# Making the normalised rows on GpSimd instead of VectorE in a two-layer gated cross-attention block

## The reference

```python
x = x + tanh(g_xattn[0]) * _L0_xattn_ref(_layernorm(x), ctx_512, ctx_512, Wc, bc)     # 16 heads of 16, then Wc
x = x + tanh(g_ffn[0])   * _L0_ffn_ref(_layernorm(x), w_gate, w_up, w_down)           # silu*up, 2:4 sparsified, down
x = x + tanh(g_xattn[1]) * _L1_xattn_ref(_layernorm(x), ctx_512, ctx_512)             # 32 heads of 8
x = x + tanh(g_ffn[1])   * _L1_ffn_ref(_layernorm(x), gate_w, gate_b, w1, w2, w3, sw1, sw2, sw3)  # 8 experts, top 2
```

## Time and profile before

| | |
|---|---|
| median of 3 runs | 654.88 us (650.46 to 657.46) |
| profiled execution | 653.18 us, its span 651.4 us |
| granted TensorE clock, mean | 0.982 of full speed |
| busy: TensorE, VectorE, ScalarE, GpSimd | 582.7, 471.9, 436.8, 238.8 us |
| instructions | 10817 |

### The profile page before, as it was taken

How to read it: one execution, slowest core, us unless ns; L and a number is a source line. 1 busy time by engine, 2 the same in 40 slices (tenths; PEclk the granted TensorE clock), 3 DMA queues, 4 the chain that set the end, 5 groups by cost and what they waited for, 6 DMA issues and landing times.

```text
span 651.4 us, 10817 instructions
## 1 busy us (share of the span) xinstructions
PE 582.7 (89%) x3552; PEld 450.7 (69%) x3552; DVE 471.9 (72%) x1152; ACT 436.8 (67%) x812; POOL 238.8 (37%) x498
## 2 busy tenths in 40 slices
PE   0654788999999999999999999999999999999886
PEld 0332576777878777777878787777778786767675
DVE  4361878686969788796969697887969696966444
ACT  3251655677786877677777868776777778678952
POOL 5340444261534334251515343351515152341120
PEclk9975999899999999999999999999999999999999
DMA  8752007000000000000000000000000000000000
GB/s 258 217 183 75 4 17 109 18 9 18 14 21 10 22 15 18 10 18 17 17 19 15 20 9 22 14 15 12 18 9 11 8 11 10 12 7 2 10 8 17
DMA packets 24694, 21.44 MB, mean 33 GB/s; under 512 B 9872, under 2 KB 23680, under 8 KB 23744
## 3 DMA queue, kind: packets, MB, share of 16 engines
q1 hardware_dynamic: 21984, 13.04, 7.8%
q0 software_dynamic: 1888, 4.87, 2.5%
q10 hardware_dynamic: 768, 2.85, 1.5%
HBM read 12.61 MB, written 5.24 MB: 27 GB/s over the span
## 4 chain that ended last, share of the span: by engine, by line
PE 66%; ACT 13%; POOL 7%; DVE 6%; issue 5%; DMA 2%; SPq 1%; DVEq 0%; POOLq 0%; ACTq 0%
PE bank L742 12%; PE bank L750 12%; PE bank L745 12%; PE bank L789 8%; PE bank L832 7%; PE bank L744 5%; PE bank L821 4%; ACT L658 3%; POOL rt L547 3%; ACT L696 2%; ACT pt L658 2%; PE bank L818 2%; PE bank L819 2%; DMA k0a<-down_hi 2%; PE bank L911 1%
## 5 line engine op out<-in xcount | busy, mean ns | idle before, releaser
L658 ACT ACTIVATE pt<-bank 128x512 f32<-128x512 f32 x192 | 109.4, 603 | 10.1 <-PE bank L821 5.5
L1092 DVE TENSOR_REDUCE mx<-bank 128x4 f32<-128x512 f32 x128 | 86.1, 684 | 8.3 <-PE bank L789 7.4
L707 ACT ACTIVATE ht_hi<-bank 128x512 fp32r<-128x512 f32 (+1 forms) x96 | 50.4, 543 | 61.4 <-PE bank L750 60.8
L742 PE MATMUL bank<-w_r,at_hi 128*128 128x352 f32 x256 | 88.4, 346 | 3.4 <-DVE work L1200 0.9
L456 POOL TENSOR_SCALAR a_ve<-a_mv 128x1 f32<-128x1 f32 x32 | 9.1, 284 | 214.2 <-DVE a_mv L1062 213.3
L745 PE MATMUL bank<-w_r,at_lo 128*128 128x352 f32 x256 | 82.2, 323 | 0.0
L1137 DVE SCALAR_TENSOR_TENSOR work<-bank,cw,work 128x176 f32<-128x176 f32 x128 | 45.3, 395 | 42.5 <-ACT work L724 28.4
L1092 DVE TENSOR_REDUCE q0b<-bank 128x4 f32<-128x512 f32 x64 | 42.6, 688 | 42.3 <-PE bank L789 42.0
L1231 DVE TENSOR_TENSOR ht_lo<-bank,ht_hi 128x512 fp32r<-128x512 f32 (+1 forms) x96 | 58.0, 618 | 18.4 <-ACT ht_hi L707 18.4
L821 PE MATMUL bank<-qt,k 128*128 128x512 f32 x128 | 54.1, 443 | 7.4 <-DMA qt<-mt 3.3
L742 PEld LDWEIGHTS bank<-w_r,at_hi 128*128 128x128 f32 x256 | 48.4, 189 | 15.3 <-DVE work L1200 5.8
(11 more groups left out here) (163 smaller groups left out, 1540.7 us busy)
## 6 DMA issues: line engine op xcount, KB each, us to landing
w_r<-in_w POOLq DMA_DIRECT2D x1, 3168.0 KB, 13.8
x<-in_x SPq DMA_DIRECT2D x16, 128.0 KB, 2.2
work<-in_w_up ACTq DMA_DIRECT2D x2, 1024.0 KB, 9.3
k<-kd SPq DMA_DIRECT2D x128, 12.0 KB
out<-y SPq DMA_DIRECT2D x16, 128.0 KB, 1.7
w_r<-in_w POOLq DMA_DIRECT2D x1, 1536.0 KB, 7.1
kd0a<-down_hi SPq DMA_DIRECT2D x2, 512.0 KB
pt<-in_w_down SPq DMA_DIRECT2D x1, 1024.0 KB, 19.3
```

The source lines that it names most:

```text
L658: act.activation(pt[:, g, :], PV[g % 2][:, :], ACT.Exp, scale=float(HD[L]) ** -0.5)\
L707: act.activation(ht_hi[:, 4 * t:4 * t + cols // P, :], DOWN[b][:, 0:cols].rearrange("p (k t) -> p k t", t=P), ACT.Copy)\
L742: pe.matmul(o, a_hi, w_hi, start=first, stop=False, skip_group_check=free)
L1092: dve.tensor_reduce(o, QK[(1 + m) % 2][:, :].rearrange("p (g t) -> p g t", t=T), AX.X, ALU.max, negate=True).then_inc(S["a_r"], step)
```

## The change

GpSimd now writes the normalised rows itself. In `rstd` the power is followed, in the same step, by the waits for the previous readers of the tile and by a `tensor_scalar` (subtract, multiply) into `a_xn` or `f_xn`. VectorE's `norm_apply` is gone, and its steps in `TIMES` stay but issue nothing. VectorE's `bn_aggr` now waits until the previous normalised rows are written, because GpSimd still reads the mean from there. No number of the table is changed. 64 instructions move from VectorE to GpSimd.

```diff
-            def rstd(pre, n, mv, ve, rs):
+            def rstd(pre, n, src, mv, ve, rs, xn):
                 wait(pool, pre + "mvd", n)
                 pool.tensor_scalar(ve[:, :], mv[:, 1:2], EPS, None, ALU.add).then_inc(S[pre + "veps"], 1)
                 yield
                 wait(pool, pre + "veps", n)
                 pool.tensor_tensor(rs[:, :], ve[:, :], neg_half[:, :], ALU.pow).then_inc(S[pre + "rstd"], 1)
+                if pre == "a_":
+                    wait_before(pool, "a_q_hi2", n)
+                    wait_before(pool, "a_q_lo", n)
+                else:
+                    wait_before(pool, "f_xt_ps", n)
+                wait(pool, pre + "rstd", n)
+                pool.tensor_scalar(xn[:, :], src[:, :], mv[:, 0:1], rs[:, :], ALU.subtract, ALU.mult)\
+                    .then_inc(S[pre + "norm"], 1)
...
-            def norm(pre, n, src, stat, mv, rs, xn):
+            def norm(pre, n, src, stat, mv):
 
                 dve.bn_stats(stat[:, :], src[:, :]).then_inc(S[pre + "stats"], 1)
                 yield
                 wait(dve, pre + "stats", n)
+                wait_before(dve, pre + "norm", n)
                 dve.bn_aggr(mv[:, :], stat[:, :]).then_inc(S[pre + "mvd"], 1)
-
-            def norm_apply(pre, n, src, mv, rs, xn):
-                wait(dve, pre + "rstd", n)
-                dve.tensor_scalar(xn[:, :], src[:, :], mv[:, 0:1], rs[:, :], ALU.subtract, ALU.mult)\
-                   .then_inc(S[pre + "norm"], 1)
...
-                yield from norm("a_", n, src, a_stat, a_mv, a_rs, a_xn)
-                yield
-                wait_before(dve, "a_q_lo", n)
-                wait_before(dve, "a_q_hi2", n)
-                norm_apply("a_", n, src, a_mv, a_rs, a_xn)
+                yield from norm("a_", n, src, a_stat, a_mv)
+                yield
```

More of the change, by code:

```diff
@@ L463, in attention_1 @@
                 n, b, c = at[L, i], at[L, i] % 2, i % 2
-                yield from rstd("a_", n, a_mv, a_ve, a_rs)
+                yield from rstd("a_", n, x0[c] if L == 0 else xr[i % NX], a_mv, a_ve, a_rs, a_xn)
                 yield
@@ L519, in ffn_1 @@
                 n, b, c = at[L, i], at[L, i] % 2, i % 2
-                yield from rstd("f_", n, f_mv, f_ve, f_rs)
+                yield from rstd("f_", n, xr[i % NX], f_mv, f_ve, f_rs, f_xn)
                 if L == 0:
@@ L1176, in ffn_1 @@
                 wait(dve, "a_out", n)
-                yield from norm("f_", n, src, f_stat, f_mv, f_rs, f_xn)
+                yield from norm("f_", n, src, f_stat, f_mv)
                 yield
-                norm_apply("f_", n, src, f_mv, f_rs, f_xn)
                 yield
```

## The result

The changed kernel takes 696.76 us (median of 4 runs) against 652.92 us for the kernel before in the same comparison: a ratio of 1.064, interval 1.057 to 1.070. It is slower by 44 us, where I had predicted 4.6 us faster and had a range that ended at 658.

The account below looks back on a forecast made before the run. TensorE was taken as the bound, some of its waits ending on norms. Terms of -0.37 us a period, times 11, and -0.5 us from warm-up gave -4.6 us: 650.3 us, range 643 to 658.

Parts of the forecast that it names:

- d: Duration of GpSimd's new normalising instruction: taken as 0.45 us, range 0.41 to 0.73, from rows of other GpSimd instructions.
- d above 0.66 us: Sign of a wrong prediction: the new instruction longer than 0.66 us, where the period was to break even.
- `lead` late: Sign of a wrong prediction: GpSimd's steps of the 2:4 choice become late and show in TensorE's waits.
- Term 1: Layer-0 attention norm, now on GpSimd: ScalarE's rounding starts about as before, -0.01 us a period, from -0.05 to +0.27.
- Term 2: Feed-forward norm at 293.82 us: rows ready earlier, TensorE's wait goes, -0.31 us a period, from -0.38 to -0.12.
- Term 3: Feed-forward norm at 314.43 us: rows slightly earlier less a conflict with VectorE, -0.05 us a period, from -0.14 to +0.18.
- Term 4: `lose` and `lead` behind the new instructions on GpSimd: nothing added to TensorE's path while d is below about 0.6 us.
- Start-up and the end: Differences before 58.06 us swallowed; warm-up to 110 us gains 0.5 us; last four layer-1 units about nothing, within 0.5 us.
- B: Rival: GpSimd's instruction stalled by VectorE instructions beside it, d about 1.2 us, +12 us, 667 us; chance 0.10.

Follow-up runs that it names:

- e8: Changed kernel with GpSimd's new instruction as multiply by 1.0 and add 0.0, leaving out the normalisation; ratio 1.007 against the kernel before.
- e6: Kernel before with one table number changed, so GpSimd adds the bias ahead of the first feed-forward norm's epsilon and power; ratio 0.998.
- e4: Kernel before plus an unread GpSimd instruction of about 1.2 us behind each of the 64 powers; 657.89 against 654.86 us, ratio 1.006.
- e2: Changed kernel with only the attention norms' rows on GpSimd, feed-forward rows back on VectorE; 675.25 us, ratio 1.035 against the kernel before.
- e3: Changed kernel with only the feed-forward norms' rows on GpSimd, attention rows back on VectorE; 674.91 us, ratio 1.034 against the kernel before.
- e9: Changed kernel with VectorE negating the mean and GpSimd doing add and multiply instead of subtract and multiply; 664.83 against 653.01 us, ratio 1.017.

## Why the prediction was wrong

The views were read rightly in the main: VectorE is not the bound, and TensorE's waits on the norms decide. In the changed kernel they still do. What failed was a price, d, and with it one place that had no term at all, the second attention norm of the period; three smaller steps failed besides. Two of the signs that I had named for a wrong prediction came: d above 0.66 us, and `lead` late. With the price as I had assumed it (e8) the ratio was 1.007, where my sum gave 0.993: most of the miss is the price, but not all.

**The price d.** I chose 0.45 us, "the kind of instruction is that of the lower row, only the type is wider". The type costs nothing; the two operations, which I took to be interchangeable, cost a factor of 2.6 (0.41 against 1.07 us), and the two scalars 0.15 us more: 1.22 us alone, 1.30 on average with its surroundings. The upper bound, 0.73 us, was no bound either: a two-input product is no dearer version of this instruction, it takes 0.61 us alone where this one takes 1.22. Both ends came from rows of the wrong operation. The factor of two that the Trainium skill gives for two-input work (GPSIMD Engine Reference, section 4.1) pointed the right way; measured it is 1.24 to 0.41, or 3.0, for this one-input pair. Its exception for one-input work, roughly line-rate, holds for the add and multiply pairs with immediates (0.41 us, as on VectorE) and fails for this one.

**Term 1, the first attention norm.** Predicted 290.39 + d for ScalarE's rounding, 0.08 us from power to rows. The wait for the engine's own result costs 0.21 us here, not the 0.08 of the step from `a_ve` to the power, and the power beside which VectorE's router steps now run takes 0.65 instead of 0.57 us. With d = 1.24 my formula gives +0.78 us; the trace has +0.98. The same two shifts make the term +0.12 us in e8, where the formula had given a gain.

**Term 2, the first feed-forward norm.** Predicted -0.31 us a period. e6 realises it without the change and the period falls by 0.10 us. I had checked ScalarE's slack at its last exponential only the earlier trace rows; the wait that took the place of the one removed stands in the middle of the row of exponentials.

**Term 3, the second feed-forward norm.** Predicted -0.05 us, with a conflict of 0.19 us "in the same spot" that compares two different places (290.40 and 314.46 us). The rows ended 0.63 us after their power (314.43 to 315.06); now it is 1.54 us (333.10 to 334.64), and TensorE waits 0.71 us.

**Term 4, what moves behind.** I wrote that it adds nothing while d is below about 0.6 and that "above, the cover shrinks". It did, and more: with d = 1.3 the norms and the 2:4 choice form one list of 8.5 us on the path. The second attention norm of the period, which I had not given a term, stands at its head: its rows end 1.43 us after their power (327.14 to 328.57) and `lose` waits behind them. e4 shows that the list's load alone is worth 0.6%, e2 and e3 that each kind of norm costs as much as the other.

**Start-up and the end.** I had expected about nothing ahead of 58 us and after 540. The parts ahead and behind grew by 8.1 and 8.7 us. The start-up itself was swallowed as predicted: TensorE's product that had started at 58.06 us starts at 54.62 (54.3 in e4, 59.5 in e9), so what was lost ahead was lost behind this point. At the end TensorE's work is thinner and each norm is on the path: the chain of the changed kernel has five instructions of L466 after 585 us, where that of before had one of L1066.

Part of both is TensorE's clock, which my sum held constant. Ahead TensorE is busy 99.4 us instead of 94.6 for the same 481 matmuls, at a mean granted clock of 0.87 instead of 0.92; behind 139.9 instead of 135.6 for the same 854, at 0.98 instead of 1.00. That is 9 us more of busy time in these parts. In which measure the later norms lowered the clock, and in which this one execution had it low by chance, is not shown.

**The rivals.** B, slower, was the right side with the right duration (1.2 us) and the wrong mechanism: I had VectorE stalling the instruction, and it takes as long alone. Its +12 us came from two places a period; the whole periods gave +25 (11 times 2.30). I had given it a chance of 0.10, because I bounded d by the two nearest rows and treated only a stall as able to leave them.

Not settled: why a wait for GpSimd's own result costs 0.18 to 0.21 us between a power and the rows and 0.08 between the epsilon and the power, and what lowers TensorE's clock outside the periods, where e8 loses 5 us.

## What to carry to other kernels

The price of a GpSimd instruction depends on its exact operation pair (0.41 or 1.07 us for the same tile): before moving elementwise work there, time the very instruction by itself at the end of a kernel, and rewrite a subtraction as an addition of the negated value. An engine that is busy 37% of the time is still not free if its result is awaited: unread work of 75 us cost 3 us here, and about as much work on the path cost 44. When you count a norm or any other step that repeats, give each of its places in the period a term, also those that no wait points to yet. When a term removes a wait, look for the next wait on the same engine before counting the gain.

## What the runs showed of the hardware

- GpSimd, 256 columns by 128 partitions, one input, alone: add and multiply, multiply and add or two multiplies 0.41 us; subtract and multiply or multiply and subtract 1.07; a single multiply 0.85, twice the price of the pair that contains it. bf16 and float32 are alike where both were run.
- Two scalars from memory in place of immediates add 0.15 us to either kind (1.07 to 1.22, 0.41 to 0.56).
- A plain product of two tiles, 0.61 us alone, is cheaper than one tile multiplied by one number: 0.85 with an immediate, 0.92 with a scalar from memory.
- TensorE's granted clock was 0.50 (1.2 GHz) for about 3 us twice in the last 30 us of e8, where it was 1.00 in the kernel before, and its 854 matmuls from the last period on kept it busy 3.0 us longer.
